# Graph layer on one core: equal destinations merged within one column of edges instead of two, scatters issued one at a time

## What is computed

```
h    = relu(LN(x))
xn   = LN(h) * g1 + b1
msg  = relu(xn[src] + edge_attr)
aggr = segment_sum(msg, dst, num_segments=N)
u    = (1 + eps_gin) * xn + aggr
u    = relu(u @ Wg1 + bg1) @ Wg2 + bg2
h2   = h + u
f    = gelu((LN(h2) * g2 + b2) @ Wf1 + bf1) @ Wf2 + bf2
out  = x + h2 + f
```

## Time and profile before

| | |
|---|---|
| median of 3 runs | 1114.41 us (1113.41 to 1115.68) |
| profiled execution, its time | 1113.83 us |
| its span | 1112.1 us |
| mean granted TensorE clock | 0.986 of full speed |
| busy: PE, PEld, DVE, ACT, POOL | 1011.0, 875.1, 939.5, 958.7, 905.6 us |
| indirect DMAs: scatters, gathers | 196 and 196 |

### The profile page before, as it was taken

How to read it: one execution, slowest core, us unless ns; L and a number is a source line. 1 busy time by engine, 2 the same in 40 slices (tenths; PEclk the granted TensorE clock), 3 DMA queues, 4 the chain that set the end, 5 groups by cost and what they waited for, 6 DMA issues and landing times. The chain is left out here.

```text
span 1112.1 us, 25459 instructions
## 1 busy us (share of the span) xinstructions
PE 1011.0 (91%) x6776; PEld 875.1 (79%) x6874; DVE 939.5 (84%) x3075; ACT 958.7 (86%) x2354; POOL 905.6 (81%) x649
## 2 busy tenths in 40 slices
PE   0325899999999999999999999999999999999998
PEld 0213688888888888888888888888888888878887
DVE  2657799899899899998998999989989989978742
ACT  0235899999999999999999999999999999989773
POOL 4378788998899889989898899899898988976720
PEclk9996899999999999999999999999999999999999
DMA  5968985555545545555455455555554554533311
GB/s 101 375 169 286 373 267 131 133 127 132 138 110 139 133 110 139 129 130 130 126 132 139 109 139 132 113 139 127 132 133 122 133 138 110 134 80 89 56 55 38
DMA packets 111416, 156.54 MB, mean 141 GB/s; under 512 B 24591, under 2 KB 51639, under 8 KB 111366
## 3 DMA queue, kind: packets, MB, share of 16 engines
q1 hardware_dynamic: 73606, 130.31, 37.6%
q0 software_dynamic: 37760, 25.66, 16.4%
HBM read 91.26 MB, written 64.61 MB: 140 GB/s over the span
## 5 line engine op out<-in xcount | busy, mean ns | idle before, releaser
L448 POOL DMA_INDIRECT aggr_sums<-e_merged,e_index x196 | 331.9, 1693 | 71.0 <-issue 43.0
L934 PEld LDWEIGHTS p_out<-wf,n_act 128*128 128x128 f32 x3136 | 365.4, 191 | 3.6
L934 PE MATMUL p_out<-wf,n_act 128*128 128x128 f32 x3136 | 365.9, 275 | 0.1
L521 ACT ACTIVATE n_act<-p_f,bf1e_col 128x512 f32<-128x512 f32 x392 | 269.3, 687 | 48.1 <-PE p_f L890 47.9
L435 POOL DMA_INDIRECT e_x<-in_x,e_cols x196 | 231.3, 1180 | 72.6 <-issue 52.8
L890 PE MATMUL p_f<-n_z2T_high,wf_low 128*128 128x512 f32 x392 | 202.2, 516 | 8.6 <-ACT n_act L521 7.6
L512 ACT ACTIVATE n_z<-n_relu,n_shift,n_rstd 128x128 f32<-128x128 f32 x392 | 161.3, 485 | 26.9 <-DVE n_shift L691 26.7
L479 POOL TENSOR_TENSOR n_rstd<-n_var,minus_half 128x8 f32<-128x8 f32 x98 | 173.4, 1769 | 4.5 <-DVE n_var L712 3.4
L487 POOL TENSOR_TENSOR n_rstd<-n_var,minus_half 128x4 f32<-128x4 f32 x98 | 145.6, 1486 | 33.9 <-DVE n_var L842 33.7
L549 ACT ACTIVATE n_h<-n_relu,n_rstd 128x128 f32<-128x128 f32 x392 | 158.8, 407 | 0.0
L890 PE MATMUL p_f<-n_z2T_low,wf_high 128*128 128x512 f32 x392 | 155.0, 395 | 0.0
(11 more groups left out here) (91 smaller groups left out, 1731.1 us busy)
## 6 DMA issues: line engine op xcount, KB each, us to landing
n_x<-in_x SPq DMA_DIRECT2D x97, 256.0 KB, 2.6
n_aggr<-aggr_sums SPq DMA_DIRECT2D x97, 256.0 KB, 3.9
out_dram<-n_out SPq DMA_DIRECT2D x97, 256.0 KB, 3.9
aggr_sums<-zeros SPq DMA_DIRECT2D x13, 1024.0 KB, 8.5
e_dst<-in_dst_rows SPq DMA_DIRECT2D x49, 256.0 KB, 4.1
e_attr<-in_attr SPq DMA_DIRECT2D x48, 256.0 KB, 2.9
aggr_sums<-zeros SPq DMA_DIRECT2D x6, 2048.0 KB, 13.8
e_x<-in_x,e_cols POOLq DMA_INDIRECT x196, 3.4
```

What stands on the lines that cost most here:

```text
L448: nc.gpsimd.indirect_dma_start(out=aggr, out_offset=bass.IndirectOffsetOnAxis(ap=e_index[0:r, s, j:j + 1], axis=0), in_=e_merged[0:r, s, j ...
L521: nc.scalar.activation(n_act[:, k, :, 0:b.rows], p_f[k % 2][:, :, 0:b.rows], ACT.Gelu, bias=bf1e_col[:, k:k + 1]).then_inc(s_act, 1)
L934: last = nc.tensor.matmul(p_out[0:b.rows, j, :], n_act[:, k, j, 0:b.rows], wf2[:, k, :], start=False, stop=(k == KF - 1), skip_group_check ...
```

## The change

PAIR becomes 1. A column is compared with itself alone, so `e_match` holds one matrix per column instead of three per pair, PE makes four products per chunk, and `later` and `e_match` shrink. Equal rows of different columns are no longer merged, so each column's scatter waits until the one before it has landed. `scatter_pair` becomes `scatter_column`, with its own wait; `gather` takes one column; and the calls in POOL's `step` are put in a new order. The other engines' programs change by PAIR alone.

```
-PAIR = 2
+PAIR = 1
...
-        PAIR_SCATTERED = 16 * PAIR
+        COLUMN_SCATTERED = 16
...
-            def scatter_pair(c, g):
+            def scatter_column(c, j):
+                if c is None:
+                    return
                 r, s = c.rows, c.slot(3)
+                if j > 0:
+                    pool.wait_ge(q_scatter[s], SCATTERED * c.uses(3) + j * COLUMN_SCATTERED)
                 pool.reg_add(bound, last_sum, 1)
-                for j in range(g * PAIR, (g + 1) * PAIR):
-                    nc.gpsimd.indirect_dma_start(
...
+                nc.gpsimd.indirect_dma_start(
...
-                if 1 in halves and not 0 in halves:
+                if halves == (1,):
                     merged_first(edge, apart)
+                if 0 in halves:
+                    scatter_column(edge(4), 2)
                 if (b := node(4)) is not None:
...
-                if 0 in halves and (c := edge(4)) is not None:
-                    pool.wait_ge(q_scatter[c.slot(3)], SCATTERED * c.uses(3) + PAIR_SCATTERED)
-                    scatter_pair(c, 1)
-                if 0 in halves and (c := edge(0)) is not None:
-                    gather(c, range(0, PAIR))
+                if 0 in halves:
+                    gather(edge(0), 0)
+                    scatter_column(edge(4), 3)
+                    gather(edge(0), 1)
...
-                if 1 in halves and (c := edge(0)) is not None:
-                    gather(c, range(PAIR, J))
+                if 1 in halves:
+                    gather(edge(0), 2)
+                    scatter_column(edge(3), 1)
+                    gather(edge(0), 3)
```

More of the change, by code:

```diff
@@ L427, in _, with gather @@
             pool.reg_mov(last_sum, AGGR_ROWS - 2)
-            def gather(c, columns):
+            def gather(c, j):
+                if c is None:
+                    return
                 r, s = c.rows, c.slot(3)
@@ L433, in gather @@
                 pool.reg_add(bound, last_node, 1)
-                for j in columns:
-                    nc.gpsimd.indirect_dma_start(
[L436 to L439, removed]
+                nc.gpsimd.indirect_dma_start(
+                    out=e_x[0:r, s, j, :], out_offset=None, in_=x,
+                    in_offset=bass.IndirectOffsetOnAxis(ap=e_cols[0:r, s, 0, j:j + 1], axis=0),
+                    bounds_check=bound,
+                ).then_inc(q_gather[s], 16)
             LAST_ZEROED = LEAD + NODE_TURN - EDGE_LAG
-            def scatter_pair(c, g):
+            def scatter_column(c, j):
+                if c is None:
+                    return
                 r, s = c.rows, c.slot(3)
+                if j > 0:
+                    pool.wait_ge(q_scatter[s], SCATTERED * c.uses(3) + j * COLUMN_SCATTERED)
                 pool.reg_add(bound, last_sum, 1)
-                for j in range(g * PAIR, (g + 1) * PAIR):
[L448 to L453, removed]
+                nc.gpsimd.indirect_dma_start(
+                    out=aggr, out_offset=bass.IndirectOffsetOnAxis(
+                        ap=e_index[0:r, s, j:j + 1], axis=0),
+                    in_=e_merged[0:r, s, j, :], in_offset=None,
+                    bounds_check=bound, compute_op=ALU.add,
+                ).then_inc(q_scatter[s], 16)
             def merged_first(edge, apart):
@@ L472, in merged_first @@
                         pool.wait_ge(q_scatter[(c.k - 1) % 3], SCATTERED * (c.value + (c.k - 1) // 3 + 1))
-                    scatter_pair(c, 0)
+                    scatter_column(c, 0)
             def step(node, edge, halves, apart):
@@ L498, in step @@
                                             ALU.pow).then_inc(s_erstd, 1)
-                if 1 in halves and 0 in halves:
+                if halves == (0, 1):
                     merged_first(edge, apart)
-                if 1 in halves and (c := edge(0)) is not None:
-                    gather(c, range(PAIR, J))
+                if 1 in halves:
+                    gather(edge(0), 2)
+                    scatter_column(edge(3), 1)
+                    gather(edge(0), 3)
             first_chunks(step, *range(LEAD))
```

## The result

The changed kernel takes 1180.13 us in the median of 4 runs (1178.61 to 1181.69), beside 1113.91 us (1112.4 to 1115.68) of the kernel before: ratio 1.0597, 95% interval 1.0574 to 1.062. Slower, as forecast, but by 66 us instead of 14, and outside the range. The profiled execution took 1181.55 us, its span is 1179.8 us, the mean granted clock 0.968 (before 0.986).

What follows compares the result with a forecast made beforehand. The prediction took TensorE to bound the kernel, with POOL keeping its beat with at most 0.3 to 0.4 us per chunk in hand. 1113.8 - 13 (middle) + 22 (start) + 5 (end) = 1127.8, so 1128 us; range 1098 to 1165.

Steps and rivals of the forecast that it cites:

- the middle: Chunks after the start, with waits: 20.05 us per chunk instead of 20.36, -13 us over 43 chunks.
- Rival 3: Middle: the second scatter keeps its 5.7 us landing, chain 21.3 us per chunk, +40 us, 1181 us in all; chance 0.13.
- Part 1: TensorE: four p_merged matmuls per chunk instead of six, 8 records instead of 12, saving 0.44 us per chunk, 18.9 us.
- Part 2: POOL's new order of single DMAs and powers, without any wait: 19.2 to 20.5 us per chunk.
- The start: Chunks 1 to 5, single-file scatters beside SP's zeros: landings of 6.0 us, 5.8 us more per chunk, +22 us.
- L479's lead: Start: L479 runs some 1.6 us ahead of its reader, so of 23 us lost +22 us reaches the other engines.
- The end: Last chunk: single-file scatters land 9.6 us later, 4.9 us of it covered before TensorE's p_in, +5 us.
- Rival 1: Whole kernel: the single file is hidden and TensorE's saving comes through, 1095 to 1100 us; chance 0.20.

Runs made afterwards that it cites:

- order of before: Kernel before with four products per chunk, columns still issued two at a time, odd ones into a buffer of their own: 1098.37 us, ratio 0.9856.
- the pair above: Kernel before and changed kernel, both with all zeros of the sums written before the first scatter: 1155.97 and 1199.43 us.
- the other order that was tried: Changed kernel with all waits, both gathers of a step ahead of its last scatter, power of 128x4 ahead of the third: 1180.59 us.

## Why the prediction was wrong

**The step that failed** is the middle, "gap by gap, the larger of POOL's own work and landing + 0.9", with its sum of 19.9 and 20.05 taken. The four distances against what was taken:

| | taken | measured |
|---|---|---|
| first to second | 4.45 | 5.18 |
| second to third | 5.1 | 5.30 |
| third to fourth | 4.45 | 4.52 |
| fourth to the next chunk | 5.9 | 6.17 |

The distances taken sum to 19.9, and the kernel without waits measures 19.94: the waits were priced at nothing, but for the 0.15 us put on top, and they cost 1.2 us per chunk. More than half of the miss is the first distance, which was priced with the median landing, 3.5. It is 5.87 us in the mean of the chunks where SP's burst comes early, which is an estimate of 5.0 for the landing. The 3.5 was right for the kernel before, where the first scatter, issued at 604.05, landed 3.5 us later, and the slow one was the second. The prediction knew that a slow landing has a fixed place, took it for a property of the second scatter, and let it fade when that moved 2.7 us away (2.5 by its own distances). With the waits it moved to the first instead, which lands in 5.0 and 5.5 us in the two runs whose traces tell. The idle time in front of the second scatter makes 0.7 of the 1.2 us; the rest is POOL's longer instructions, which the prediction did not have.

One error of method stands behind the number. A larger-of-two with a margin of 0.05 us on one side (4.45 against 4.4) has no expected gain: any spread of the landing can only lengthen it, and the spread was there to read, 3.3 to 5.9. That a wait costs its length on POOL was right, since POOL has no idle time but issue: 0.7 us per chunk over 43 chunks is 30 us.

**Rival 3** had the time (1181 against 1180) by luck: its +40 for the middle is 8 too much, its +22 for the start 8 too little. It had the size of the chain (21.3 against 21.2) by the wrong place: no wait at the third scatter, a wait at the second. Its mechanism, a scatter that lands slowly because SP's traffic surrounds it, is only half shown: moving or shortening two of these transfers gave back 8 us each, and the slow landing goes with the moment of SP's burst, but it does not stay with the second scatter whatever POOL does.

**Part 1** held: 8 records, and 15.4 us (order of before) to 19.5 us (no waits) of the 18.9. **Part 2** held for the run without waits, 19.94. But its upper end was real too: in the run whose second scatter doesn't wait POOL has no idle time for a landing and takes 20.53.

**The start** was right in its mechanism (POOL waits for a landing ahead of most second to fourth scatters there) and 8 us short. From chunk 1 to chunk 5 it took 113.4 us, 28.3 per chunk, with 27.6 forecast. The rest is 3.8 us already lost at chunk 1 (72.40 for 68.57), which the prediction had not counted, and the 1.6 us credited to L479's lead. Some 24 of the 30 us are the zeros' doing, as the pair above shows.

**The end** was right: the scatters stand 8.2 us apart (7.3 + 0.9). Block 96, on DVE and TensorE:

```profile
1130.55 0.69 DVE L831 TENSOR_TENSOR n_in<-n_zg,n_aggr 128x512 f32<-128x512 f32 x1 [3.10 <-DMA n_aggr<-aggr_sums]
```

```profile
1132.55 0.60 PE L932 MATMUL p_in<-ident,n_in 128*128 128x128 f32 x4
```

From the last chunk's first scatter n_in comes after 34.8 us instead of 25.4, 9.4 later with 9.6 forecast, and p_in after 36.8 instead of 30.9, 5.9 with 5 forecast.

**Rival 1** fell on both counts, the start and the middle. The Trainium skill, "DMA: Bandwidth & Descriptors", section "Anatomy of one DMA — SWDGE (gpsimd) path", puts the fixed part of such a DMA at about 2.0 us and calls it nearly constant. With its rate for the bytes and the 1.65 us of issue that is an estimate of 3.8 us from the start of the issue. The traces come near it for the quick landings (3.3 to 3.5) and lie above it for the first scatter beside SP's traffic (5.0 in the mean with the gather ahead), beside the zeros (up to 9.5) and in the tail (7.3).

## What to carry to other kernels

Before putting a wait for a landing on an engine, look whether that engine has idle time to pay it from. POOL had none but its issue time, so some 0.7 us of wait per chunk went into every engine's beat; one gather moved ahead, so that POOL's own work covered the landing, took 41 us off in the run where only one scatter waits. An engine that waits for late data, as DVE did here, shows how the delay travels and not where it is paid. When operations go in single file, add up landing plus hand-over over the whole cycle and compare with the cycle; here 0.7 us was left, and the other order that was tried gained nothing. Fewer links (two columns together) gave the loss back, but no gain. Where the larger of two nearly equal times is taken, count the spread of both as cost, and let a landing that was slow in one place be slow wherever the same traffic meets it.

## What the runs showed that was not expected

- The distance from the first scatter to the second varies from chunk to chunk between 4.3 and 6.2 us, and TensorE's beat with it (19.9 to 24.1), although every chunk issues the same instructions. It goes with SP issuing its loads 0.9 or 1.6 us after the first scatter.
- POOL's own instructions are 0.5 to 0.6 us per chunk longer in the runs with waits than in the one without, also where no wait shows as idle time.
- A scatter waiting for another's landing starts about 0.9 us after it: calm or busy, 3.5 or 7.3 us of landing.
- A power of 128x4 on POOL took between 1.04 and 1.75 us in different places, so distances from start to start in one order are no prices for another.
